# Second edge stage of a graph network with expert gating: block and row numbers staged by ScalarE, destination logits picked in bfloat16

## What is computed

```python
h = (x_flat @ W_gat).reshape(M, HEADS, NUM_EXPERTS)
a_src = (h * att_src).sum(-1)
a_dst = (h * att_dst).sum(-1)
e = leaky_relu(a_src[src] + a_dst[dst], negative_slope=0.2)
e_max = segment_max(e, dst, num_segments=M)
ee = exp(e - e_max[dst])
denom = segment_sum(ee, dst, num_segments=M)
agg = segment_sum(h[src] * (ee / denom[dst])[:, :, None], dst, num_segments=M)
scores = layernorm(agg).mean(heads);  top-2 gates;  out = sum_e gate_e * expert_e(x)
```

## Time and profile before

| | us |
|---|---|
| plain runs, median of 3 | 4171.85 (4165.95 to 4173.73) |
| profiled execution: span of the trace | 5269.4 |
| PE busy / PEld busy | 3476.8 / 2890.9 |
| DVE busy | 3039.4 |
| ACT busy | 1492.7 |
| POOL busy | 2649.1 |
| granted PE clock over the span, mean | 0.769 |

### The profile page before, as it was taken

The page is one execution under the profiler, slowest core; times in us unless marked ns, Lnnn a source line. Parts: engine busy times, 40 slices in busy tenths (PEclk is TensorE's granted clock), DMA queues, the critical chain, the costliest instruction groups (busy, mean ns, idle before and its releaser), DMA issues. The chain is left out here.

```text
span 5269.4 us, 87248 instructions
## 1 busy us (share of the span) xinstructions
PE 3476.8 (66%) x16727; PEld 2890.9 (55%) x16728; DVE 3039.4 (58%) x9074; ACT 1492.7 (28%) x4965; POOL 2649.1 (50%) x2767
## 2 busy tenths in 40 slices
PE   5555555665566665666655537888888888888860
PEld 4444444444454444444444436777777777777760
DVE  5566655555565666666666665555555555555558
ACT  3222222222222222222222213333333333333310
POOL 1555555555555555555555522555555555555540
PEclk9777777777777777777777766888888888888865
DMA  5322333332333333333332242111111111111118
GB/s 121 82 78 75 84 82 81 84 84 79 82 82 99 101 101 102 100 101 101 101 84 78 77 79 49 20 20 22 20 20 22 20 20 22 20 21 21 20 16 239
DMA packets 224394, 356.43 MB, mean 68 GB/s; under 512 B 65743, under 2 KB 143761, under 8 KB 224051
## 3 DMA queue, kind: packets, MB, share of 16 engines
q0 software_dynamic: 114560, 234.67, 19.2%
q1 hardware_dynamic: 100624, 109.13, 7.5%
q10 hardware_dynamic: 8867, 9.05, 0.6%
HBM read 294.17 MB, written 45.66 MB: 64 GB/s over the span
## 5 line engine op out<-in xcount | busy, mean ns | idle before, releaser
L791 POOL DMA_INDIRECT msg<-table,idx x1680 | 1630.7, 971 | 1305.1 <-ACT rel L806 844.6
L1466 POOL DMA_INDIRECT xmsg<-xtable,xidx x1060 | 1002.8, 946 | 889.0 <-ACT xidx L1482 589.7
L1159 PE MATMUL psS_e<-msg,hot 128*125 128x260 f32 x3360 | 1182.9, 513 | 281.4 <-issue 162.2
L1159 PEld LDWEIGHTS psS_e<-msg,hot 128*125 128x125 f32 x3360 | 815.5, 254 | 512.3 <-issue 337.3
L888 DVE TENSOR_TENSOR room<-room,psS_e 125x260 f32 x842 | 356.5, 423 | 361.7 <-remote 180.9
L1024 DVE TENSOR_TENSOR msg<-msg,psW_e 128x1024 f32<-128x1024 f32 x420 | 509.5, 1213 | 8.8 <-issue 1.1
L812 ACT CAST hotT<-psT_e 125x512 bf16<-125x512 f32 x422 | 244.7, 580 | 951.6 <-remote 649.7
L1012 DVE TENSOR_REDUCE look<-psD_e 128x32 f32<-128x96 f32 x420 | 106.6, 254 | 700.7 <-remote 553.8
L1076 PE MATMUL psD_e<-ad_b,hotT 125*128 x1684 | 133.9, 182 | 559.8 <-issue 151.3
L1655 PE MATMUL psY<-w,hid 128*125 128x256 f32 x1600 | 457.1, 447 | 56.7 <-issue 29.6
L1065 PEld LDWEIGHTS psT_e<-ident,hot 128*125 128x125 f32 x1692 | 320.7, 240 | 248.2 <-ACT hotT L812 157.7
(11 more groups left out here) (308 smaller groups left out, 4436.9 us busy)
## 6 DMA issues: line engine op xcount, KB each, us to landing
msg<-table,idx POOLq DMA_INDIRECT x1680
experts_out<-y_room SPq DMA_DIRECT2D x101, 224.0 KB
y_back<-experts_out SPq DMA_DIRECT2D x25, 896.0 KB
xmsg<-xtable,xidx POOLq DMA_INDIRECT x1060
xs<-x_all SPq DMA_DIRECT2D x100, 125.0 KB
table<-hrow SPq DMA_DIRECT2D x50, 113.8 KB
x_all<-in_x SPq DMA_DIRECT2D x5, 1120.0 KB
xin<-in_x SPq DMA_DIRECT2D x50, 112.0 KB
```

The costliest lines, as they stand in the source:

```text
L791: nc.gpsimd.indirect_dma_start(msg[:, u, j, :], None, table[:, :], bass.IndirectOffsetOnAxis(ap=idx[:, u, j:j + 1], axis=0)).then_inc(gath ...
L1159: last = nc.tensor.matmul(psS[:, u % 2, j // GT, 0:ROW], hot[:, u, j, :], msg[:, u, j, :], start=j % GT == 0, stop=j % GT == GT - 1)
L1466: nc.gpsimd.indirect_dma_start(msg[:, u, j, :], None, xtable[:, :], bass.IndirectOffsetOnAxis(ap=idx[:, u, j:j + 1], axis=0)).then_inc(gat ...
```

## The change

- ACT stages two more rings: `xlo` (the row numbers, a copy) and `xhi_rel` (the block number plus `cls_rel[k]`, an Identity activation with a pointer bias). The semaphore `staged` now follows the last of the three. XAHEAD is 4 in place of 3.
- DVE no longer reads `step_i`: the one-hot takes `xlo`, and waits for `staged`; the two comparisons take `xhi_rel` and have no pointer scalar.
- `xad_all` is split once, ahead of the steps, into three bfloat16 parts (`xad_b`) whose sum is the float32 value. `xhotT` is bfloat16. A pick is four bfloat16 products of 120 columns in place of four float32 products of 40. `xprod` has 480 elements in place of 160, and the sum to `xlook` runs over 15 terms in place of 5.

```diff
-XAHEAD = 3
+XAHEAD = 4
...
-    CF = CB * 2 * XH
+    XP = 3 * 2 * XH
+    CF = CB * XP
...
+        lo = sb("xlo", [P, XRING, XT])
+        hi_rel = sb("xhi_rel", [P, XRING, XT])
...
-        hotT = sb("xhotT", [NB, 3, XT, P])
+        hotT = sb("xhotT", [NB, 3, XT, P], BF16)
+        xad_b = sb("xad_b", [NB, BLOCKS, 3, 2 * XH], BF16)
...
-        prod = sb("xprod", [P, XT, CB, 2 * XH])
+        prod = sb("xprod", [P, XT, CB, XP])
...
             def stage(k, w):
                 at = step_at(act, k)
-                nc.scalar.copy(idx[:, RING[w], :], xs_i[:, bass.ds(at, 1), :].rearrange("p a j -> p (a j)")) \
-                    .then_inc(staged, 1)
+                nc.scalar.copy(idx[:, RING[w], :], xs_i[:, bass.ds(at, 1), :].rearrange("p a j -> p (a j)"))
+                nc.scalar.copy(lo[:, RING[w], :], lo_all[:, bass.ds(at, 1), :].rearrange("p a j -> p (a j)"))
+                nc.scalar.activation(hi_rel[:, RING[w], :], hi_all[:, bass.ds(at, 1), :].rearrange("p a j -> p (a j)"),
+                                     ACT.Identity, bias=cls_rel[:, bass.ds(k, 1)]).then_inc(staged, 1)
...
+            left = prod[0:NB].rearrange("p j b f -> p (j b f)")[:, 0:BLOCKS * 2 * XH] \
+                .rearrange("p (b f) -> p b f", b=BLOCKS)
+            split = Chain(dve, xad_split)
+            split.link(V.tensor_copy(left, xad_all))
+            three_parts(nc, split, left, xad_b)
...
             def one_hot(k, w):
-                at = step_at(dve, k)
-                V.tensor_tensor(hot[:, RING[w], :, :], bcast(node_p, 1, XT),
-                                bcast(lo_all[:, bass.ds(at, 1), :].rearrange("p a j -> p (a j)"), 2, NB),
+                dve.wait_ge(staged, k + 1)
+                V.tensor_tensor(hot[:, RING[w], :, :], bcast(node_p, 1, XT), bcast(lo[:, RING[w], :], 2, NB),
                                 ALU.is_equal).then_inc(hot_ready, 1)
...
-                at = step_at(dve, k)
                 ch = Chain(dve, chain, PER * k)
-                blk = bcast(hi_all[:, bass.ds(at, 1), :].rearrange("p a j -> p (a j)"), 2, CB)
-                first_of = cls_rel[:, bass.ds(k, 1)]
-                ch.also(V.scalar_tensor_tensor(hi[:], blk, first_of, bcast(bid_p, 1, XT), ALU.add, ALU.is_equal))
+                blk = bcast(hi_rel[:, u, :], 2, CB)
+                ch.also(V.tensor_tensor(hi[:], bcast(bid_p, 1, XT), blk, ALU.is_equal))
...
-                ch.link(V.reduce_sum(look[:], prod[:].rearrange("p j b f -> p j f b"), AX_X))
+                ch.link(V.reduce_sum(look[:], prod[:].rearrange("p j b (s f) -> p j f (b s)", s=3), AX_X))
...
-                                            xad_all[:, bass.ds(c * CB, CB), :].rearrange("p b f -> p (b f)"),
+                                            xad_b[:, bass.ds(c * CB, CB)].rearrange("p b s f -> p (b s f)"),
...
+            pe.wait_ge(xad_split, 6)
             pick(0, 0)
```

More of the change, by code:

```diff
@@ L1394, in gating_sums_and_experts @@
         iotas_kept = sem("iotas_kept")
+        xad_split = sem("xad_split")
         chain = sem("chain_g")
@@ L1553, in step @@
                 u = RING[w % SPAN]
-                at = step_at(dve, k)
                 ch = Chain(dve, chain, PER * k)
-                blk = bcast(hi_all[:, bass.ds(at, 1), :].rearrange("p a j -> p (a j)"), 2, CB)
-                first_of = cls_rel[:, bass.ds(k, 1)]
-                ch.also(V.scalar_tensor_tensor(hi[:], blk, first_of, bcast(bid_p, 1, XT), ALU.add, ALU.is_equal))
+                blk = bcast(hi_rel[:, u, :], 2, CB)
+                ch.also(V.tensor_tensor(hi[:], bcast(bid_p, 1, XT), blk, ALU.is_equal))
                 if not first:
                     dve.wait_ge(widened, k)
-                ch.link(V.scalar_tensor_tensor(hi_p, blk, first_of, bcast(bid_p, 1, XT), ALU.add, ALU.is_equal))
+                ch.link(V.tensor_tensor(hi_p, bcast(bid_p, 1, XT), blk, ALU.is_equal))
                 dve.wait_ge(dst_picked, k + 1)
                 V.tensor_tensor(prod[:], psD[:, 0:XT * CF].rearrange("p (j b f) -> p j b f", j=XT, b=CB),
-                                bcast(hi[:], 3, 2 * XH), ALU.mult).then_inc(picked_read, 1)
+                                bcast(hi[:], 3, XP), ALU.mult).then_inc(picked_read, 1)
                 dve.wait_ge(picked_read, k + 1)
-                ch.link(V.reduce_sum(look[:], prod[:].rearrange("p j b f -> p j f b"), AX_X))
+                ch.link(V.reduce_sum(look[:], prod[:].rearrange("p j b (s f) -> p j f (b s)", s=3), AX_X))
                 dve.wait_ge(gathered[u], (visit * RING.count(u) + (w // XRING + 1)) * (16 * XT))
```

## The result

The changed kernel takes **3972.5 us** (median of 4 runs, 3966.32 to 4022.45); the kernel before, on the same chip, 4170.0 (4165.95 to 4173.73). The ratio is 0.9549 (95% interval 0.9497 to 0.9601): 197.5 us less. The forecast was 61 us less, 4111, with a range of 4025 to 4200; the sign is right, the size is not.

The account below looks back on a forecast made before the run. The second edge stage was taken as paced by DVE in four of ten intervals, by ACT and PE in six. DVE's -29 us and the middle pairs' -32 sum to -61, 4172 to 4111 us, range 4025 to 4200.

Parts of the forecast that it names:

- four intervals of ten: Second edge stage: DVE paces four of a trip's ten intervals and the 15 last steps, ACT and PE the other six.
- The floor from the gathers: Second edge stage: gathers' busy time plus issue, 1302 us, allow no less than 4.91 us a step.
- The net term on DVE: DVE, second stage: reads saved less added elements, -0.25 us a step over 115 steps, -29 us.
- interval 0-1: DVE's step 0 to 1 of a loop trip, 5.39 us before, should be near 5.14 us after.
- The loop's jump stays: DVE's gap at the second stage's loop jump, 3.29 us a trip, was expected to remain.
- the middle pairs' -32: Six middle intervals, 75 pairs with a Gelu group: one pick saved (-0.77), staging charged (+0.34), -0.43 us each, -32 us.
- PE's and ACT's terms: Second stage: a pick falls from 1.19 to 0.42 us on PE; ACT's staging ends 0.34 us later, at 0.53.
- At nothing: Priced at zero: splitting xad_all, the one-hot's wait for staging (about a microsecond left), and earlier gathers through XAHEAD = 4.
- B: Rival: PE alone paces the middle intervals, both picks of a pair count, 145 us less, 4027 us; chance 0.15.
- C: Rival: DVE's longer sum costs three times as much, 1.32 us; no change, 4170 us; chance 0.12.
- D: Rival: a loop of exponential, staging, Gelu and logits paces all four Gelu pairs; +59 us, 4231 us; chance 0.12.
- E: Rival: PE idles more and more second-product groups run at the lower clock; +76 us, 4248 us; chance 0.06.

Follow-up runs that it names:

- e0_before: The kernel before the change, unedited, run and profiled once more: 4172.23 us.
- e2_parts: The kernel before with only the three bfloat16 parts added; DVE's reads of step_i and XAHEAD = 3 as before, no new rings: 4378.88 us.
- e3_reads_kept: The changed kernel with DVE's two reads of step_i left in each step, values unused: 4304.17 us.
- e8: The kernel of e6_parts_in_psum with ACT's Gelu group moved ahead of the copy of the turned one-hot and the staging: 3913.73 us.
- e9: The changed kernel with ACT's Gelu group moved ahead of the copy of the turned one-hot and the staging: 3915.47 us.
- e5_padded: The changed kernel with eight increments of an unused semaphore added to each DVE step, no read of step_i: 4033.52 us.
- e1_rings: The changed kernel with float32 picks, xprod of 160 elements and sum of 160 terms as before; rings and XAHEAD = 4 stay: 3979.24 us.
- e4_ahead3: The changed kernel with XAHEAD = 3 in place of 4: 4469.72 us.
- e6_parts_in_psum: The changed kernel with the three bfloat16 parts added up by PE in PSUM, twelve picks of 40 columns, 160 elements on DVE: 3939.04 us.

## Why the prediction was wrong

**The bound.** Right in size: a plain step at DVE's own pace of 6.0 us, measured 5.97. Wrong in the step behind it, that four intervals of ten go by DVE and "six by a loop of ACT and PE". That came from waits in an execution 1098 us too long, the same waits that the prediction had refused to use as prices. The undisturbed trace has DVE pacing nearly all 265 steps, shown by `e0_before`, `e2_parts` and `e3_reads_kept`. What lengthened that execution stays open; DVE's busy time is the same in both (3039.4 and 3037.5 us), so on DVE it is the waits that grew. The floor from the gathers, 4.91 us a step, was sound: `e8` and `e9` end at 5.00.

**The net term on DVE: -0.25 us a step forecast, -0.68 measured.** The pieces (the table's rows over 262 to 265 steps): one-hot's read -0.73 (forecast -0.66); the read ahead of `xhi`, without the jump, (254.2 - 74) / 263 = -0.68 (forecast -0.49); the comparisons -0.18 (put at nothing, without a reason; seen in the rows alone, no run changes only them); `xprod` +0.33 and the sum +0.58 (forecast +0.33 and +0.57). An interval 0-1, forecast at 5.14 us, takes 4.82. The read ahead of `xhi` was priced from one row of 0.52; its idle time goes up to 0.86 in other steps of the trip. And idle time leaves something out: an instruction without a read starts 0.08 us ahead of the end of the one before it (0.10 after the start of a logit that takes 0.18), so a read that shows as idle time costs that and this overlap. What shows depends on what stands ahead of it: the third read, of the class, stands behind the four instructions of the spread, and `e0_before` has only 14.8 us of "issue" ahead of `acc`.

**The jump.** "The loop's jump stays" was the step that failed outright: 74 us. It was read as a property of the loop, when it depends on the length of DVE's body (`e5_padded`), and the removed reads are part of that body.

**The sum.** From -61 us: the forecast net on 265 steps in place of 115, -37; the net's size, 0.43 x 265, -114; the jump, -74; the middle pairs' -32 do not exist, +32; the new wait for the exponential, +57. That gives -197.

**PE's and ACT's terms** were about right in size (a pick of 0.38 us, a staging of 0.53) and wrong in place: the pick was not on the path, as `e2_parts` shows. Its use is the opposite of what was credited: it keeps PE from holding DVE up once DVE is faster, and DVE pays for it, so `e1_rings` and the change end level.

**At nothing.** The one-hot's new wait is hidden as argued (0.7 us in all), and `e4_ahead3` shows how thin that cover was. The split into parts showed no cost: the first `xhi` starts at 2449.2 us, before at 2449.9.

**The rivals.** B's 4027 came nearest, by a mechanism that is not there. C's threefold sum did not come (1017 ns). D's wait for the exponential did come, 85 us against 33.7, as what remains after the gain, not as the bound; in `e1_rings` and `e6_parts_in_psum` it is a bound. E did not come: PE's clock in the stage is 0.98 of 2.4 GHz in the mean, where `e0_before` shows 0.91 with more work on PE:

```profile
2470.00:4000.00 1530.00, 1397.50 (x8293) 1276.59 (x8292) 962.68 (x3681) 681.88 (x1387) 966.89 (x1023) 0.91 0.15 24
```

What it feared is seen in `e2_parts`, where the picks are short and the step is longer: PE is busy for 76% there, its clock is 0.85, and a second product takes 462 ns in the mean where `e0_before` has 404. DVE set the pace there, so the time does not show what that cost:

```profile
2470.00:4200.00 1730.00, 1320.90 (x7245) 1139.95 (x7244) 1188.54 (x3667) 668.63 (x1382) 961.39 (x1020) 0.85 0.13 21
```

## What to carry to other kernels

When a profiled execution is much longer than the plain runs, take no bound from its waits: have it profiled again, or price both with and without them. A register read inside a loop costs its idle time, the lost overlap, and a share of the loop body; one behind long instructions shows little idle time. Follow the gap at the jump and the instruction queue's bytes to see whether the body is refetched each trip. Each relief is worth its full amount only down to the next engine's pace (here PE and ACT at 5.1 to 5.3 us a step, then the gathers at 5.00), so look up these paces first.

## What the hardware showed unexpectedly

- A loop body of DVE that is too long (some 356 instructions; at some 325 there was none of it) has some 3 us of idle time at every jump (70.1 us in 23 jumps of `e5_padded`) and 40 KB of instructions, without any operation that the profile names.
- Twelve bfloat16 picks of 40 columns, with their weight loads, take 0.46 us, four of 120 columns 0.38, and four in float32 of 40 columns, as eight records, 0.98: splitting columns and accumulating costs PE 0.08 us and saves DVE 0.91.
- The comparison with a pointer scalar costs 235 ns, with a staged operand 172.
